# Second attention joined to the dense stage before it in one program, with the split stacks stored in rows of 4,098 bytes

## The chip, the cores and the metric

One NeuronCore of a Trainium2 chip runs the whole kernel in one launch. The metric is the device time of an execution in microseconds (us). The kernel before takes 2052.94 us (median of 3 runs, 2052.21 to 2053.58).

## What is computed

Two transformer layers over x of 8 batches x 512 positions x 128 channels, each `x = layernorm(x + f(x))` twice:

```python
x = _layernorm(x + _L0_attn_ref(...))   # relative-position attention, 16 heads of 8 channels
x = _layernorm(x + _L0_ffn_ref(...))    # r * (relu(xk W_k)^2 W_v), r = sigmoid(xr W_r)
x = _layernorm(x + _L1_attn_ref(...))   # the second attention
x = _layernorm(x + _L1_ffn_ref(...))    # gated MLP, 512 hidden units
# second attention, for each of the 16 heads of each batch:
term1 = einsum('bhqd,bhkd->bhqk', Q, K)
term2 = einsum('bhqd,kd->bhqk', Q, r)             # r: sines and cosines of the distance
term3 = einsum('hd,bhkd->bhk', u, K)[:, :, None, :]
term4 = einsum('hd,kd->hk', v, r)[None, :, None, :]
scores = (term1 + term3 + _rel_shift(term2 + term4)) / sqrt(dk)
out = einsum('bhqk,bhkd->bqhd', softmax(scores), V)
```

The shift leaves a few scores beside the diagonal that the product of split rows doesn't give; they come from a correction, the "edge" below.

## The kernel before, in words

The program is a chain of phases: `opening_phase` (projections of the first attention), `attention_phase(0)`, `mixing_phase` (output product, two layer norms, first feed-forward part, and the projections of the second attention), `attention_phase(1)` and `dense_phase`. This text calls `mixing_phase` the mixing stage. Between two phases stand two blocks of their own. `end_phase` clears every semaphore that the phase used, one instruction each on SyncE (line 89), and `start_phase` raises every semaphore of the next phase by 32, again one instruction each (line 81). Every block ends in a barrier of all engines. Each engine has its own program, written by hand in the order in which it runs; waits are on semaphores. SyncE (SP) issues all DMAs from one queue, in its program's order, and a wait on it holds back whatever is behind.

**Mixing stage.** It goes in steps (`STEPS`, from -3 to 7), and a step works on up to four batches at once: `a` (first residual), `m` (feed-forward), `p` (second norm and projections) and `tail`, the batch whose queries, keys and rotated queries are split. For `tail`, VectorE (DVE) runs `spin` and `rotate` (lines 1372 to 1381), and then three bf16 parts are made of five rows of 512 per channel: ScalarE (ACT) `high` (L1237), DVE `remainder` (L1387), ACT `middle` (L1242), DVE `low` (L1392). The halves of `full` are `HALVES[0]` (keys and both queries) and `HALVES[1]` (rotated queries). SP then stores them by `write_stacks` to `stack[1]` in HBM: 15 DMAs a batch (L1051, L1057), in rows of 512 bf16 values (1 KB), since keys and the four query arrays lie apart. `high(b, 0)` waits until the stores of batch b - 2 have landed. At its end SP waits for all stores (L1107).

**Second attention.** 128 heads, one after another, four tiles of 128 queries each. SP loads a head's rows with four DMAs (`head_load`, L532 to 535) into one of 8 slots, 8 heads ahead. TensorE (PE) makes the head's edge product (`edge`, L761), DVE copies it (`edge_out`, L848) to one of two `corr` buffers, SP writes it to `shear_e` (L577) and reads it back skewed into one of four `band` buffers (`edge_read`, L584); this is done for 5 heads before the first tile. For each tile PE makes the scores (L703, L705), DVE adds the band (`finish`, L835) and takes the row maximum (L843), ACT makes the exponentials (L906), PE turns them (L724), ACT copies them (L913). PE weighs the values for four heads at a time (L737). The first `FIRST` = 4 heads stand before the loop.

```python
            if left >= CORR_AHEAD - 1:
                hold(sp, added, 4 * (n + CORR_AHEAD - bands))
                edge_read(sp, Head(i, j + CORR_AHEAD - 1))
```

## Time and profile before

| what | value |
|---|---|
| three runs | 2052.21, 2052.94, 2053.58 us |
| the profiled execution's own time | 2053.05 us |
| its span | 2051.2 us, 44474 instructions |
| granted TensorE clock, mean | 0.937 |
| busy share of the span | PE 84%, DVE 71%, ACT 72%, POOL 4% |
| DMA | 404.65 MB, 197 GB/s over the span |

The profile comes from one execution. The first attention runs from about 105 to 897 us of the span, the mixing stage from 907 to 1085, the second attention from 1092 to 1699, the dense phase from 1704 to the end. A busy share is an average over stages that have different limits, so the rows of one stage say more than the table. In the slices of the page a digit is the busy share of a 51 us slice in tenths.

### The profile page before, as it was taken

Reading aid. Unit: us, or ns where it says so; the run is one execution under the profiler, and the core shown is the slowest. Engines: PE = TensorE matmul, PEld = TensorE weight load, DVE = VectorE, ACT = ScalarE, POOL = GpSimd, SP = SyncE. Lnnn points to the kernel's source line nnn. Section 1 sums busy time; section 2 is a strip of 40 time slices with the busy share of each in tenths; the row PEclk is TensorE's granted clock in tenths of the full one; section 3 lists DMA queues with packets and bytes.
Section 4 is the critical chain, followed back from the end, with each engine's and each line's share of the span. In section 5 each row is a group of like instructions: output and inputs, shape, how many; then the busy total and the mean of one; then the engine's idle time right before and its main releaser. Section 6 shows DMA issues by size and latency. Waiting matters only on the chain. (4 is left out here: it accounts for less than half of the span.)

```text
span 2051.2 us, 44474 instructions
## 1 busy us (share of the span) xinstructions
PE 1728.5 (84%) x11694; PEld 1042.4 (51%) x11694; DVE 1454.1 (71%) x3499; ACT 1472.5 (72%) x2600; POOL 79.9 (4%) x102
## 2 busy tenths in 40 slices
PE   5269999999999999946743999999999995999998
PEld 2045555555555555524522555656565552454544
DVE  6358888888888888837973888988888873324322
ACT  4348888888888888836862999999999991223222
POOL 0000000000000000003510000000000000000000
PEclk8569999999999999977875999999999997999999
DMA  7678888888888888726996777777777744000100
GB/s 229 214 222 257 265 269 267 264 261 266 262 264 268 266 266 261 240 56 184 327 311 182 206 213 210 215 211 214 212 211 211 212 136 117 22 20 26 36 5 11
DMA packets 428234, 404.65 MB, mean 197 GB/s; under 512 B 38169, under 2 KB 348433, under 8 KB 428049
## 3 DMA queue, kind: packets, MB, share of 16 engines
q1 hardware_dynamic: 428177, 403.99, 65.6%
q8 instruction: 24, 0.39, 0.1%
q14 instruction: 33, 0.27, 0.0%
HBM read 227.09 MB, written 176.29 MB: 197 GB/s over the span
## 5 line engine op out<-in xcount | busy, mean ns | idle before, releaser
L906 ACT ACTIVATE a_prob<-bank,a_negmax 128x512 f32<-128x512 f32 x1024 | 740.8, 723 | 47.3 <-DVE a_negmax L843 46.1
L843 DVE TENSOR_REDUCE a_negmax<-bank 128x1 f32<-128x512 f32 x1024 | 699.4, 683 | 0.3
L724 PE MATMUL bank<-a_ident,a_prob 128*128 128x128 f32 x4096 | 643.0, 280 | 56.2 <-ACT a_probt L913 48.3
L913 ACT COPY a_probt<-bank 128x512 f32<-128x512 f32 x1024 | 621.3, 607 | 90.4 <-PE bank L724 79.1
L724 PEld LDWEIGHTS bank<-a_ident,a_prob 128*128 128x128 f32 x4096 | 448.5, 141 | 171.7 <-issue 70.6
L835 DVE TENSOR_TENSOR bank<-bank,a_band 128x128 f32<-128x128 f32 (+3 forms) x1024 | 349.9, 342 | 69.6 <-PE bank L705 69.0
L703 PE MATMUL bank<-a_stks 74*128 74x192 bf16 (+7 forms) x1024 | 324.1, 317 | 10.4 <-ACT a_prob L906 10.1
L737 PE MATMUL bank<-a_probt,a_vs 128*32 128x512 f32 x2048 | 271.5, 604 | 14.9 <-ACT a_probt L913 14.9
L823 DVE COPY_PREDICATED bank<-a_mask,bank 128x128 f32<-128x128 uint32 (+1 forms) x512 | 139.6, 273 | 116.4 <-PE bank L709 114.0
L703 PEld LDWEIGHTS bank<-a_stks 74*128 74x128 bf16 (+1 forms) x1024 | 100.1, 98 | 235.3 <-ACT a_prob L906 200.4
L705 PE MATMUL bank<-a_stks 74*128 74x320 bf16 (+5 forms) x768 | 200.9, 262 | 0.0
L1676 DVE TENSOR_TENSOR d_drop<-bank,d_s 128x128 f32<-128x128 f32 x32 | 7.1, 284 | 170.4 <-PE bank L1599 170.4
L709 PE MATMUL bank<-a_stks 74*128 74x128 bf16 (+1 forms) x512 | 110.5, 216 | 10.9 <-DVE bank L823 2.6
L1578 PE MATMUL bank<-d_ha,d_h1T 128*128 128x512 f32 x256 | 112.3, 592 | 0.0
L751 PE MATMUL bank<-a_ident,a_sheared 128*128 128x128 f32 x512 | 106.4, 285 | 6.6 <-DMA a_sheared<-shear_a 5.1
L1578 PE MATMUL bank<-d_hb,d_h2T 128*128 128x512 f32 x256 | 111.2, 592 | 0.0
L925 ACT COPY a_corr<-bank 128x512 f32<-128x512 f32 x128 | 76.4, 597 | 42.9 <-PE bank L752 40.1
L848 DVE COPY a_corr<-bank 128x512 f32<-128x512 f32 x128 | 87.2, 681 | 16.7 <-PE bank L761 9.3
L752 PE MATMUL bank<-a_tabs,a_stks 65*128 65x128 bf16 x512 | 97.5, 225 | 0.0
L853 DVE COPY a_keyside<-bank 128x512 f32<-128x512 f32 x128 | 87.4, 683 | 13.3 <-PE bank L744 10.4
L761 PE MATMUL bank<-edges,a_stks 96*128 96x128 bf16 x512 | 51.0, 223 | 50.1 <-DMA a_ident<-in_ident 42.5
L1641 ACT ACTIVATE d_hb<-bank,d_fs 128x512 f32<-128x512 f32 x32 | 22.0, 687 | 90.6 <-PE bank L1578 90.6
(178 smaller groups left out, 1594.7 us busy)
## 6 DMA issues: line engine op xcount, KB each, us to landing
a_band<-shear_b SPq DMA_DIRECT2D x128, 512.0 KB, 5.0
shear_a<-a_keyside SPq DMA_DIRECT2D x128, 256.0 KB, 3.7
a_sheared<-shear_a SPq DMA_DIRECT2D x128, 256.0 KB, 3.7
shear_b<-a_corr SPq DMA_DIRECT2D x128, 256.0 KB, 2.8
shear_e<-a_corr SPq DMA_DIRECT2D x128, 256.0 KB, 2.2
a_band<-shear_e SPq DMA_DIRECT2D x128, 256.0 KB, 3.2
a_stks<-stack SPq DMA_DIRECT2D x256, 96.0 KB, 3.0
a_stks<-stack SPq DMA_DIRECT2D x384, 48.0 KB, 2.6
```

The costliest lines, as they stand in the source:

```text
L703: last = pe.matmul(score[:, 0:c], k[:, qlo, q], k[:, keys, 0:c], start=True, stop=True)
L705: last = pe.matmul(score[:, c:T], k[:, qhi, q], k[:, keys, c:T], start=True, stop=True)
L709: last = pe.matmul(other[:, 0:e - a], k[:, qhi, q], k[:, keys, a:e], start=True, stop=True)
L724: last = pe.transpose(turned_bank[k][:, n * 128:(n + 1) * 128], prob[h.slot % 2][:, n, k * 128:(k + 1) * 128], ident[:, :])
L737: pe.matmul(cbank[32 * j:32 * j + VW, :], vs[g][:, at:at + VW], probt[h.slot + j][:, k, :], start=(k == 0), stop=(k == NT - 1)).then_inc(p ...
L751: pe.matmul(corr_bank[:, q], sheared[h.slot % 4][:, q], ident[:, :], is_transpose=True, start=True, stop=False)
L823: v.copy_predicated(score[:, a:e], mask[:, 0:e - a], other[:, 0:e - a]).then_inc(fixed, 1)
L835: v.tensor_tensor(score[:, a:e], score[:, a:e], band[h.slot % bands][:, n, w:w + e - a], ALU.add).then_inc(added, 1)
L843: v.tensor_reduce(negmax[h.slot % 2][:, n:n + 1], score[:, :], AX.X, ALU.max, negate=True).then_inc(maxed, 1)
L906: nc.scalar.activation(prob[h.slot % 2][:, n, :], score[:, :], ACT.Exp, bias=negmax[h.slot % 2][:, n:n + 1]).then_inc(exped, 1)
L913: nc.scalar.copy(probt[h.slot][:, k, :], turned_bank[k][:, :]).then_inc(copied, 1)
L1578: last = pe.matmul(dst[:, :], w[:, k, 128 * m:128 * m + 128], src[:, k, :], start=(k == 0), stop=(k == KH - 1))
```

## The change

The mixing stage and the second attention become one block with one `start_phase` ahead of it and one `end_phase` behind it. `mixing` and `attention` are now functions that give back a `Stage`, whose `program` writes the engines' parts one behind the other into the same block. To fit in memory, most tiles of the mixing stage lie in an `arena` whose bytes the attention's `prob` and `probt` tiles use later. Bands and `corr` buffers of the second attention are 8 and 8 instead of 4 and 2. The first 5 heads' edge products, copies (now on ACT), writes and reads, the first 8 heads' loads, the key positions and the first values are issued inside the mixing steps. The last batch's stacks are stored between the attention's first four heads (`store_last`), and SP waits for all stores of the mixing stage (`settled`) before the attention's loop. `stack[1]` is laid out anew: keys first, then both queries and both rotated queries side by side, so that a batch is stored by 3 DMAs of 1 KB rows and 3 DMAs of 4,098-byte rows instead of 15 of 1 KB rows; a row of the stack is 5,184 bytes from the next instead of 5,120.

```diff
-ARRAYS = 5
+PITCH_S = 5 * T + 32
...
-                wide, bands = WIN if rel else REL, 4
+            wide, bands, corrs = (WIN, 4, 2) if rel else (REL, 8, 8)
...
+            def edge(pe, h, target):
+                pe.wait_ge(stk_in[h.slot], BASE + per_stk * (h.i + 1))
...
+            def first_edge(pe, j):
+                pe.wait_ge(corr_copied, BASE + j - 1)
+                edge(pe, Head(0, j), first_banks[j % 2])
+            def first_edge_out(act, j):
+                act.wait_ge(corr_mm, BASE + j + 1)
+                nc.scalar.copy(corr[j][:, :, :], first_banks[j % 2][:, :].rearrange("p (n r) -> p n r", n=NT)).then_inc(corr_copied, 1)
...
                         for j in range(FIRST):
                             sync_step(sp, 0, j, NHEAD, weighed=False)
+                        if not rel:
+                            mix.store_last(sp, j)
+                    if not rel:
+                        mix.settled(sp)
...
                     @block.tensor
                     def _(pe):
                         if not rel:
-                            pe.wait_ge(s_const, BASE + 16)
-                        if not rel:
-                            for j in range(CORR_AHEAD):
-                                edge(pe, Head(0, j))
+                        mix.banks_free(pe)
                             pe.wait_ge(poskey_in, BASE + 16)
...
-                        else:
-                            for j in range(CORR_AHEAD):
-                                edge_out(v, Head(0, j))
...
+            def write_queries(sp, b, run):
+                sp.wait_ge(lo_set, BASE + 2 * b + 2)
+                first_term, n, q = TERM_RUNS[run]
+                same = bass.AP(part[b % 2][:, :, :].tensor, q * (WIDE + 2) + QV, [[3 * (WIDE + 2), C], [0, n], [1, 4 * T + 1]])
+                sp.dma_start(stack[1][b, :, first_term:first_term + n, T:5 * T + 1], same).then_inc(stack_written[b % 2], 16)
+            def store_last(sp, j):
+                if j < len(TERM_RUNS):
+                    write_queries(sp, B - 1, j)
+                else:
+                    write_keys(sp, B - 1)
+            def banks_free(pe):
+                for done in (q_out, qs_out, key_out, v_out, relu_done, summed1, turn2, gated):
+                    pe.wait_ge(done, BASE + B)
...
                             if p is not None:
                                 store_rows(p)
+                        if tail == 6:
+                            for j in range(CORR_AHEAD):
+                                att.edge_write(sp, j)
                             if tail is not None:
                                 write_values(tail)
-                                write_stacks(tail)
+                        if tail == 6:
+                            for j in range(CORR_AHEAD - 1):
+                                att.edge_read(sp, j)
+                        if tail == 7:
+                            att.edge_read(sp, CORR_AHEAD - 1)
+                        if tail is not None and tail < B - 1:
+                            write_keys(sp, tail)
+                            for run in range(len(TERM_RUNS)):
+                                write_queries(sp, tail, run)
+                        if tail == 1:
+                            att.first_poskey(sp)
+                        if tail == 2:
+                            sp.wait_ge(v_written[0], BASE + 16)
+                            sp.wait_ge(stack_written[0], BASE + 16 * N_STACK)
...
+                            att.first_values(sp)
+                        if tail in (2, 3, 4, 5):
+                            att.head_load(sp, 2 * tail - 4)
+                            att.head_load(sp, 2 * tail - 3)
```

In the step with `tail` = 6, PE runs `first_edge` 2 and 3 behind `flip_rows2` and `first_edge` 4 between `queries` and `keys`; `first_edge` 0 and 1 end the step before. ACT runs `first_edge_out` 0 and 1 behind `rows2`, 2 and 3 behind `turned2`, and 4 behind `middle(6, 0)`.

Two places in the order of the instructions. On ACT, in the step with `tail` = 6, the kernel before has (L1258 is `rows2` of batch 7, L1237 `high`, L1270 `turned2`, L1242 `middle`, L1210 to L1214 `queries_out`):

```order
L1258 ACTIVATE m_x21<-m_pre2,m_shift,m_rstd 128x128 x4
L1237 CAST m_part0<-m_full0 128x1024
L1270 COPY m_xt2<-bank5 128x512
L1242 CAST m_part0<-m_left 128x1538
L1210 ACTIVATE m_qv<-bank0,m_uvs 128x512
L1211 ACTIVATE m_full1<-bank0,m_uvs 128x512
L1214 ACTIVATE m_full1<-bank1,m_uvs 128x512
L1242 CAST m_part0<-m_left 128x1024
```

and the changed kernel, whose mixing tiles are named after the arena they lie in:

```order
L1322 ACTIVATE m_x21<-arena,m_shift,m_rstd 128x128 x4
L655 COPY a1_corr0<-bank6 128x512
L655 COPY a1_corr1<-bank4 128x512
L1301 CAST m_part0<-arena 128x1024
L1334 COPY arena<-bank5 128x512
L655 COPY a1_corr2<-bank6 128x512
L655 COPY a1_corr3<-bank4 128x512
L1306 CAST m_part0<-arena 128x1536
L655 COPY a1_corr4<-bank6 128x512
L1274 ACTIVATE arena<-bank0,m_uvs 128x512
L1275 ACTIVATE arena<-bank0,m_uvs 128x512
L1278 ACTIVATE arena<-bank1,m_uvs 128x512
```

Five copies have come in ahead of `queries_out`. On SP, at the end of the mixing stage, the kernel before stores the last batch and goes through the change of phase (L89 clears semaphores) to the first head's load:

```order
L1051 DMA stack1<-m_part1 128x512
L1057 DMA stack1<-m_part1 128x512 x4
L1017 UNCONDITIONAL_BRANCH
L86 UNCONDITIONAL_BRANCH
L89 ISA x67
L85 UNCONDITIONAL_BRANCH
L78 UNCONDITIONAL_BRANCH
L77 UNCONDITIONAL_BRANCH
L629 UNCONDITIONAL_BRANCH
L532 DMA a1_stks<-stack1 48x1536
```

and in the changed kernel the edge writes and reads of the first heads stand in the mixing step with `tail` = 6, ahead of that batch's stores (L1035 keys, L1042 queries):

```order
L1097 DMA resid<-m_x21 128x4x128
L582 DMA shear_e<-a1_corr0 128x4x128
L582 DMA shear_e<-a1_corr1 128x4x128
L582 DMA shear_e<-a1_corr2 128x4x128
L582 DMA shear_e<-a1_corr3 128x4x128
L582 DMA shear_e<-a1_corr4 128x4x128
L1092 DMA values<-m_vt0 128x4x144
L589 DMA a1_band0<-shear_e 128x4x128
L589 DMA a1_band1<-shear_e 128x4x128
L589 DMA a1_band2<-shear_e 128x4x128
L589 DMA a1_band3<-shear_e 128x4x128
L1035 DMA stack1<-m_part0 128x3x512
```

The loads of the first eight heads have moved further up, to the steps with `tail` = 2 to 5, behind those steps' stores.

## Rows read from the trace of the kernel before

**Rows 1.** The page, part 1: busy time of each engine over the span.
```profile
PE 1728.5 (84%) x11694; PEld 1042.4 (51%) x11694; DVE 1454.1 (71%) x3499; ACT 1472.5 (72%) x2600; POOL 79.9 (4%) x102
```
**Rows 2.** Windows: start:end, length, busy by engine, then PEclk, DMA share, GB/s.
```profile
1060.00:1070.00 10.00, 0.00 (x0) 0.00 (x0) 7.95 (x8) 4.94 (x4) 0.00 (x0) 0.51 0.99 338
1110.00:1120.00 10.00, 7.03 (x32) 4.29 (x33) 7.41 (x18) 5.47 (x9) 0.00 (x0) 0.50 0.85 230
1300.00:1400.00 100.00, 94.55 (x788) 60.45 (x784) 88.89 (x203) 98.45 (x185) 0.00 (x0) 1.00 0.73 214
```
**Rows 3.** Timeline of DVE at the change of phase: start, us, line, operation, idle before.
```profile
1057.32 1.23 DVE L1392 TENSOR_TENSOR m_part<-m_left,m_part 128x1024 bf16<-128x1024 f32 x1 [2.12 <-ACT m_part L1242]
1058.46 0.68 DVE L1372 TENSOR_TENSOR m_rot<-m_qv,m_trig 128x512 f32<-128x512 f32 x1
...
1065.49 2.90 DVE L1392 TENSOR_TENSOR m_part<-m_left,m_part 128x1538 bf16<-128x1538 f32 x2 [0.41 <-ACT m_part L1242]
1092.45 0.11 DVE L858 MEMSET a_vs<- 128x23 f32 x2 [24.07 <-PEq L77]
...
1112.68 0.49 DVE L835 TENSOR_TENSOR bank<-bank,a_band 128x128 f32<-128x128 f32 x2
```
**Rows 4.** Clears (L89) and increments (L81) of semaphores on SP at two changes of phase.
```profile
L81 SPq EVENT_SEMAPHORE  x67: 17/17/17, 903.0 to 906.9; - x67
L89 SPq EVENT_SEMAPHORE_RANGE_CLEAR  x67: 25/25/29, 1085.9 to 1089.5; - x67
```
**Rows 5.** Timeline of DVE, first `spin` product of two steps that follow each other.
```profile
1000.69 0.69 DVE L1372 TENSOR_TENSOR m_rot<-m_qv,m_trig 128x512 f32<-128x512 f32 x1
1015.87 0.69 DVE L1372 TENSOR_TENSOR m_rot<-m_qv,m_trig 128x512 f32<-128x512 f32 x1
```
**Rows 6.** Timeline of ACT in the step with tail 6, and `high(7, 0)` behind it.
```profile
1047.79 1.65 ACT L1258 ACTIVATE m_x<-m_pre,m_shift,m_rstd 128x128 f32<-128x128 f32 x4 [0.66 <-POOL m_shift L1313]
1050.26 1.04 ACT L1237 CAST m_part<-m_full 128x1024 bf16<-128x1024 f32 x1 [0.83 <-DVE m_full L1381]
1053.96 0.69 ACT L1210 ACTIVATE m_qv<-bank,m_uvs 128x512 f32<-128x512 f32 x1 [0.55 <-PE bank L1155]
1056.25 1.03 ACT L1242 CAST m_part<-m_left 128x1024 bf16<-128x1024 f32 x1
1060.15 1.47 ACT L1237 CAST m_part<-m_full 128x1538 bf16<-128x1538 f32 x1 [1.46 <-DMA stack<-m_part]
```
**Rows 7.** Timeline of PE: queries of batch 7, an edge product at the same clock.
```profile
1051.85 2.07 PE L1155 MATMUL bank<-m_xt,m_wq 128*128 128x512 f32 x2 [1.25 <-ACT m_xt L1270]
1053.71 1.92 PE L1157 MATMUL bank<-m_xt,m_wqs 128*128 128x512 f32 x2
1101.93 0.61 PE L761 MATMUL bank<-edges,a_stks 96*128 96x128 bf16 x4 [0.79 <-DVE a_corr L848]
```
**Rows 8.** The page, part 5: an ACT copy of 128x512 out of PSUM.
```profile
L913 ACT COPY a_probt<-bank 128x512 f32<-128x512 f32 x1024 | 621.3, 607 | 90.4 <-PE bank L724 79.1
```
**Rows 9.** Timeline of SP: first store of batch 5, batch 7's residual, last stores.
```profile
1046.52 0.37 SPq L1051 DMA_DIRECT2D stack<-m_part  x1
...
1058.06 0.46 SPq L1061 DMA_DIRECT2D resid<-m_x  x1
...
1081.71 2.19 SPq L1057 DMA_DIRECT2D stack<-m_part  x4
```
**Rows 10.** Windows: 1 KB stores alone, opening stores with rows to 6 KB, 512-byte zeros.
```profile
1070.00:1083.00 13.00, 0.00 (x0) 0.00 (x0) 0.00 (x0) 0.00 (x0) 0.00 (x0) 0.50 1.00 342
49.00:52.00 3.00, 2.53 (x4) 0.70 (x5) 2.96 (x5) 1.26 (x3) 0.00 (x0) 0.65 1.04 407
936.00:941.00 5.00, 4.94 (x28) 3.50 (x26) 2.93 (x11) 2.64 (x4) 2.54 (x4) 0.86 1.05 291
```
**Rows 11.** The page, part 6: band reads, KB each, us from issue to landing.
```profile
a_band<-shear_e SPq DMA_DIRECT2D x128, 256.0 KB, 3.2
```
**Rows 12.** One tile (a_stks), 1085 to 1140 us: issue time in ns, min/median/max.
```profile
L533 SPq DMA_DIRECT2D a_stks<-stack x12: 414/424/2032, 1092.8 to 1137.5; - x12
```

More of the change, by code:

```diff
@@ L415, in _, with attention @@
                         offset_low(B - 1)
-        def attention_phase(layer, kept=None):
+        class Stage:
+            pass
+        def attention(layer, ctx, kept):
             rel = layer == 0
@@ new lines, in attention @@
+            else:
+                arena, ident = kept
+                stks = sb("stks", [R1, unroll, 4, T], BF16)
+                tiles = arena.rearrange("p (i n t) -> p i n t", n=NT, t=T)
+                prob, probt = [tiles[:, i] for i in range(2)], [tiles[:, 2 + i] for i in range(unroll)]
+            stk = [stks[:, i] for i in range(unroll)]
+            vs = [sb(f"vs{i}", [128, GROUP * NT * VC + VW - VC]) for i in range(vslots)]
+            negmax = [sb(f"negmax{i}", [128, NT]) for i in range(2)]
@@ new lines, in attention @@
+            outs = sb("outs", [128, T])
+            wide, bands, corrs = (WIN, 4, 2) if rel else (REL, 8, 8)
+            corr = [sb(f"corr{i}", [128, NT, REL]) for i in range(corrs)]
+            band = [sb(f"band{i}", [128, NT, wide]) for i in range(bands)]
+            if rel:
+                mask = sb("mask", [128, 128], U32)
+                tab = [tabs[:, i] for i in range(unroll)]
+                keyside = [sb(f"keyside{i}", [128, T]) for i in range(4)]
+                sheared = [sb(f"sheared{i}", [128, T]) for i in range(4)]
@@ new lines, in first_poskey, with first_values @@
+            def first_poskey(sp):
+                every = bass.AP(waves[:, :].tensor, 0, [[T, SR], [0, unroll], [1, T]])
+                sp.dma_start(stks[SR:R1, :, KEY, :], every).then_inc(poskey_in, 16)
+            def first_values(sp):
+                for g in range(vslots):
+                    sp.dma_start(vs[g][:, 0:GROUP * NT * VC], values[g]).then_inc(v_in[g], 16)
+            def edge(pe, h, target):
+                pe.wait_ge(stk_in[h.slot], BASE + per_stk * (h.i + 1))
+                for n in range(NT):
+                    q = slice(128 * n, 128 * n + 128)
+                    last = pe.matmul(target[:, q], stk[h.slot][:, EDGE, q], edges[:, :], start=True, stop=True)
+                last.then_inc(corr_mm, 1)
@@ new lines, in scalar_step @@
+                            if left >= (k + exp_ahead) // NT:
+                                exp_tile(act, *ahead(i, j, k, exp_ahead))
+                            copy_turned(act, own, k)
+                            if k == 1 and weighed and j % GROUP == GROUP - 1:
+                                group_out(act, Head(i, j - j % GROUP - GROUP))
+                        if rel and left >= CORR_AHEAD:
+                            corr_out(act, Head(i, j + CORR_AHEAD))
+                    for j in range(FIRST):
+                        scalar_step(0, j, NHEAD, weighed=False)
@@ new lines, in _ @@
+                    with act.Fori(0, loops) as i:
+                        for j in range(unroll):
+                            scalar_step(i, FIRST + j, NHEAD)
+                    for j in range(last):
+                        scalar_step(loops, FIRST + j, last - 1 - j)
+                    group_out(act, Head(loops, FIRST + last - GROUP))
+            stage = Stage()
+            stage.head_load, stage.edge_write, stage.edge_read = ((lambda sp, j, move=move: move(sp, Head(0, j)))
+                                                                  for move in (head_load, edge_write, edge_read))
@@ L1719, in build @@
             end_phase()
-            attention_phase(0, kept)
-            end_phase()
-        mixing_phase()
-        end_phase()
-        attention_phase(1)
+            with ExitStack() as ctx:
+                att = attention(0, ctx, kept)
+                start_phase()
+                with nc.Block() as block:
+                    att.program(block)
+            end_phase()
+        with ExitStack() as ctx:
+            arena = ctx.enter_context(nc.sbuf_tensor("arena", [128, (2 + UNROLL[1]) * NT * T], F32))
+            ident = ctx.enter_context(nc.sbuf_tensor("ident", [128, 128], F32))
+            att = attention(1, ctx, (arena, ident))
+            mix = mixing(ctx, arena, ident, att)
+            start_phase()
+            with nc.Block() as block:
+                mix.program(block)
+                att.program(block, mix)
         end_phase()
```

1661 lines of the change are left out of this document (818 added, 843 removed).

## The prediction

> **What bounds the kernel now.** I read the page first: PE is busy for 84% of the span, DVE and ACT for some 72% [rows 1], so there is idle time, and the question is where. The windows give it by stage. Inside the second attention ACT is busy for 98.45 of 100 us at a granted clock of 1.00 (2.4 GHz) [rows 2]: that stage is ACT's, and nothing in the change makes ACT's work there shorter. Between 1060 and 1070 us PE is idle, DVE and ACT finish the last split, and DMA is at 0.99 of its share [rows 2]. The timeline of DVE then shows the hole: the last `low` of the mixing stage ends at 1065.49 + 2.90 = 1068.39, and the first tile of the second attention is finished from 1112.68 on, **44.3 us** later [rows 3]. In that hole lie the stores of the last two batches (to 1083.9) [rows 9], the clears and increments of semaphores [rows 4], the loads of the first heads and their edge corrections. DVE and ACT stand on both sides of it, so the hole is on the path whole.
>
> Inside the mixing stage the steps follow each other every 15.2 us [rows 5]. DVE has hardly a gap there, and DMA is nearly full too, so I treat both as limits and check below which of them the changed kernel meets.
>
> **1. The hole goes: -44.3 us, +0.2.** The second attention's programs now stand behind the mixing stage's in the same block. DVE goes from its last `low` to two memsets (0.11 us together [rows 3]) and the first `finish`. That one needs four things: PE's scores (banks free once ACT has copied batch 7's values, about 10 us earlier), the loaded heads and key positions (issued two to five steps earlier), and band 0. I find all of them ready; band 0 is the latest, and is worked out in part 3. The ramp behind the first tile has the same work as before. PE went through it at a granted clock of 0.50, 1.2 GHz, after the idle stretch at 0.51 [rows 2], and I expect the same again.
>
> **2. Five edge copies on ACT: +3.1 us.** They came off DVE's start of the attention, inside the hole, and now stand ahead of `queries_out` in the step with `tail` = 6. ACT was at 1.04 us of cast from 1050.26, and started `queries_out` at 1053.96 [rows 6]. A copy takes 0.61 us [rows 8]. Copies 0 and 1 fit mostly into the 0.83 us in which ACT waited for DVE; `turned2` then ends at about 1052.2. PE, at 0.61 us for an edge product, runs edge 2 and 3 before `queries`, starts these at 1052.2 and, as their two products took 2.07 and 1.92 us from 1051.85 on [rows 7], reaches edge 4 at about 1056.2 and ends it at 1056.8. Copy 4 waits for that on ACT, and `queries_out` for copy 4: start at 1057.5. Three activations of 0.6 on, the second `middle` starts at 1059.4, where it was at 1056.25 [rows 6]: +3.1. DVE's `low` waited for exactly this one (2.12 us [rows 3]), and all of DVE's work for batch 7 follows it, so it is on the path. Bounds: 0, if PE is faster and ACT's waits hide the copies; 4.5, five copies and an edge product and a half. The rest of `tail` = 7 keeps its length. The 1.46 us that ACT waited for a store before `high(7, 0)` [rows 6] was not on the path: DVE was busy until 1062.
>
> **3. The stores and what SP now carries: 0 us.** A batch's stack is 15 DMAs or 3840 KB, 3.93 MB. SP issues them at the pace at which they flow: 1046.5 to 1058.0, 11.5 us [rows 9], or 342 GB/s in the stretch with stores of 1 KB rows alone [rows 10]. Four fifths of the bytes (3.15 MB) now go in rows of 4,098. The nearest rows are the opening phase's stores, in rows of 1 to 6 KB: 407 GB/s [rows 10]. I take 400, which gives 7.9 us for these and 2.3 us for the keys at 342: 10.2 us a batch, 1.3 less. The lower bound is the 291 GB/s of 512-byte zeros and loads [rows 10]: 13.5 us a batch, 2.0 more.
> In the steps 2 to 5 SP has eight more issues each, for two heads. At 0.42 to 0.5 us [rows 12] that is 3.8 us, more than their bytes need. Stores, loads and the residual and value DMAs (1.0 us) make 15.0 us, just under the 15.2 of the step. So store 5 starts about where it did, 0.5 us late, ends at 1057.2 and SP is through the loads at 1061. `high(7, 0)`, now at 1061.6, doesn't wait. Residual, five edge writes and the values take 3.3 us more. The read of band 0 goes out at about 1064.8 and, with 3.2 us to landing [rows 11] and a full queue, lands by 1069. DVE arrives at 1071.5. So the cover is 2.5 us; when it is gone, what is late next is band 0, and behind it `high(7, 0)`.
> Band 4 is read a whole store later, near 1076, but is due only 16 tiles on. The last batch's stack (3.93 MB) goes out during four heads of about 5.9 us, which carry some 0.8 MB of their own each: 7.1 MB at 342 are 21 us in 23.6. Bands are read four heads ahead; I cost it at nothing.
>
> **4. Semaphores: +6.7 us.** The instructions that clear and raise them don't go away; the hole only held some of them. The merged program has 109 semaphores (67 and 42; the attention alone had 32). Increments cost 3.9 us for 67, or 0.059 each, and clears 3.6 us for 67, or 0.054 [rows 4]. Ahead of the mixing stage there are 42 more: +2.5. Behind the attention there are 77 more clears: +4.2. Both stand where all engines wait.
>
> **5. Edits costed at nothing.** DVE's edge copies with 8 buffers instead of 2 wait less, in a stage that ACT bounds. The far rotated rows are read in 1 KB rather than 2 KB pieces, under a DMA share of 0.73 [rows 2]. `settled` on SP waits some 3 us, with bands and heads several heads ahead. The arena changes addresses, not instructions.
>
> **Sum.** -44.3 + 0.2 + 3.1 + 0 + 6.7 = -34.3 us against the profiled execution's 2053.05 us: **2018.8 us**. The median of the runs is 0.1 us lower, so no correction is due.
>
> **The rivals.**
> *A. DMA holds the mixing stage's end: the long rows are no faster.* For it: DMA is already at 0.99 to 1.00 of its share there [rows 2, 10]. Against it: 407 GB/s in the opening. At 342 each store is 1.3 us longer; over the steps 1 to 5, with SP's extra issues, store 5 starts 4 us late, band 0 lands near 1074 instead of 1069, and DVE waits 2.5: 2021.3. At 291, store 5 ends at 1070, `high(7, 0)` is late too and band 0 lands at 1082: 2029.3. The Trainium skill, DMA: Bandwidth & Descriptors, section "Where 436 GB/s comes from", says that for transfers between HBM and SBUF a core's share of HBM, about 358 GB/s, binds. By that rule this rival would hold, near its first time. The trace disagrees for short stretches: 3 us at 407 GB/s.
> *B. The attention starts on time but starves.* Stores of batch 7 delay the head loads and bands on SP's one queue. The last band before the stores has a slack of many us, the bytes fit only at 90%. If one head's worth of work is lost: +5.9, 2024.7.
> *C. Slower than before: the 4,098-byte rows are slow ones.* Their last 2 bytes are a piece of their own kind, and rows begin on multiples of 64 bytes only. Six stores stand ahead of band 0 on SP's queue, and the step has no room left, so each us more per store costs six. The change loses once they take 34.3 / 6 = 5.7 us more each, 3.15 MB in 13.6 us, or 231 GB/s. At half of the measured 342 they take 18.4 us, band 0 comes 55 us later than I have it, and the time is about 2073. Against it: no row moves that slowly in a full queue; even 512-byte pieces reach 291.
> *D. The overlap doesn't come about.* Some wait (the banks, the key positions) holds the attention back to the end of all stores, near 1084: 12 us lost, 2031. Against it: the code's waits name only batch-7 products that are ten us old.
>
> **How the numbers follow.** Forecast (parts 1 to 4, DMA with cover) 0.62; A at 342 to 291 0.18; B 0.08; D 0.07; C 0.05. The forecast's own bounds are 2015.7 (edge copies free) and 2020.2 (copies at 4.5), and PE may come into the ramp nearer its last work and at the higher clock, which I put at 1 to 2 us less: 2014. The range goes to 2028, over B and most of A, and leaves out D, C and the worst of A: about 0.15. All cases but C are faster by over 0.2% (4 us, about what a measurement of this kernel tells from no change): faster 0.95, within 0.2% 0.01, slower 0.04.
>
> **What would show it.** Right: DVE's gap between the last `low` and the first `finish` under 1 us; `queries_out` of batch 7 behind copy 4, 3 us later against `rows2` of batch 7; stores of a batch in 10 us; 109 increments over 6.4 us ahead of the mixing stage and 109 clears over 5.9 behind the attention; the attention's steady stage unchanged at ACT 98%. Wrong: a wait for `a_band` or for `stack<-m_part` at the joint (A), mixing steps longer than 15.2 us (A or C), ACT under 95% in the first heads (B), or a gap of over 10 us on DVE (D).

## The result, and the profile after

The changed kernel takes **2025.26 us** (median of 4 runs, 2023.52 to 2025.86), against 2053.01 for the kernel before beside it: ratio 0.9862, 95% interval 0.9849 to 0.9875. Faster, as forecast, and inside the range, but 27.8 us are gained where the forecast was 34.3. The profiled execution (2025.06 us, span 2023.3, granted clock 0.945) is the one read here.

I cut both executions at the same places. "Ahead" reaches from SP's first clear behind the first attention to the first of the last eight `spin`s, "mixing" from there to the end of the last `low`, "gap" to the first `finish`, "attention" to SP's first clear behind it, "rest" to the end of the span.

| us | opening, first attention | ahead | mixing | gap | second attention | rest | span |
|---|---|---|---|---|---|---|---|
| before | 899.7 | 54.2 | 114.5 | 44.3 | 587.3 | 351.2 | 2051.2 |
| after | 899.1 | 56.5 | 117.2 | 0.0 | 593.4 | 357.1 | 2023.3 |
| difference | -0.6 | +2.3 | +2.8 | -44.3 | +6.1 | +5.9 | -27.9 |

The timeline of DVE over the change of program (start, us, line, operation, idle before it) answers [rows 3]:

```profile
1061.80 1.23 DVE L1464 TENSOR_TENSOR m_part<-arena,m_part 128x1024 bf16<-128x1024 f32 x1 [3.46 <-ACT m_part L1306]
1062.94 0.69 DVE L1444 TENSOR_TENSOR arena<-arena 128x512 f32<-128x512 f32 x1
...
1069.97 2.90 DVE L1464 TENSOR_TENSOR m_part<-arena,m_part 128x1536 bf16<-128x1536 f32 x2 [0.40 <-ACT m_part L1306]
...
1072.84 0.27 DVE L838 TENSOR_TENSOR bank<-bank,a_band 128x128 f32<-128x128 f32 x1
```

The hole of 44.3 us is gone to the last tenth: the first `finish` (L838) starts at 1072.84, as the last `low` (L1464) ends. But 20 us on, DVE stands still, and again behind that (same columns):

```profile
1094.80 0.30 DVE L838 TENSOR_TENSOR bank<-bank,a_band 128x128 f32<-128x128 f32 x1 [3.12 <-DMA a_band<-shear_e]
1100.52 0.30 DVE L838 TENSOR_TENSOR bank<-bank,a_band 128x128 f32<-128x128 f32 x1 [1.84 <-PE bank L719]
1112.50 0.30 DVE L838 TENSOR_TENSOR bank<-bank,a_band 128x128 f32<-128x128 f32 x1 [3.63 <-DMA a_band<-shear_e]
```

It waits for bands 5 and 8 to land (heads are counted from 0, four `finish` each). SP's timeline shows where they were (issues, us, line; the waits of SP are the gaps between rows):

```profile
1085.44 0.43 SPq L1042 DMA_DIRECT2D stack<-m_part  x1
1086.83 0.38 SPq L582 DMA_DIRECT2D shear_e<-a_corr  x1
1087.33 1.30 SPq L589 DMA_DIRECT2D a_band<-shear_e  x1
...
1101.49 1.68 SPq L1035 DMA_DIRECT2D stack<-m_part  x3
1107.25 0.37 SPq L582 DMA_DIRECT2D shear_e<-a_corr  x1
1108.00 0.37 SPq L589 DMA_DIRECT2D a_band<-shear_e  x1
```

Band 5's read (L589) is issued at 1087.33, behind a store of 1,537 KB (L1042) of 1085.44, and DVE has it 7.5 us later. Band 8's read comes after the stores of the keys and after `settled`, in which SP waited for all stores of the stack (the waits of SP's queue, 1072 to 1130: us in total, times, longest):

```profile
SPq L522 <- DVE a_corr L851: 9.5, 5, 6.4
SPq L1057 <- DMA stack<-m_part: 3.6, 1, 3.6
```

The windows (PE, PEld, DVE, ACT busy us and instructions, POOL, granted clock, DMA share, GB/s) show what it does to ACT, which bounds this stage. They answer to [rows 2]:

```profile
1080.00:1090.00 10.00, 9.46 (x70) 6.16 (x67) 9.22 (x23) 9.86 (x19) 0.00 (x0) 0.98 0.97 333
1090.00:1100.00 10.00, 7.21 (x43) 3.25 (x43) 5.56 (x13) 7.53 (x14) 0.00 (x0) 0.87 1.05 327
...
1110.00:1120.00 10.00, 6.84 (x46) 4.00 (x44) 5.71 (x14) 5.57 (x11) 0.00 (x0) 0.83 0.73 209
1300.00:1400.00 100.00, 94.08 (x783) 59.73 (x782) 88.11 (x202) 98.11 (x185) 0.00 (x0) 1.00 0.73 212
```

9.86 of 10 us while the bands that were read in the mixing stage last, 7.53 and 5.57 in the two windows with the waits, and 98 of 100 later, as in the kernel before. PE's clock falls to 0.87 and 0.83 in the windows in which it ran dry.

The semaphores stand as counted (one line of code: duration ns, first and last start; increments L81, clears L89), to be read beside [rows 4]:

```profile
L81 SPq EVENT_SEMAPHORE  x109: 17/17/17, 902.4 to 909.1; - x109
L89 SPq EVENT_SEMAPHORE_RANGE_CLEAR  x109: 25/25/49, 1666.2 to 1672.7; - x109
```

6.7 and 6.5 us. And ACT in the step with `tail` = 6, which answers to [rows 6]:

```profile
1050.18 1.65 ACT L1322 ACTIVATE m_x<-arena,m_shift,m_rstd 128x128 f32<-128x128 f32 x4 [0.66 <-POOL m_shift L1385]
1051.73 1.04 ACT L655 COPY a_corr<-bank 128x512 f32<-128x512 f32 x2
...
1054.10 1.07 ACT L655 COPY a_corr<-bank 128x512 f32<-128x512 f32 x2
1055.05 1.49 ACT L1306 CAST m_part<-arena 128x1536 bf16<-128x1536 f32 x1
1058.50 0.58 ACT L655 COPY a_corr<-bank 128x512 f32<-128x512 f32 x1 [1.96 <-PE bank L646]
1058.98 0.69 ACT L1274 ACTIVATE arena<-bank,m_uvs 128x512 f32<-128x512 f32 x1
```

From `rows2` to `queries_out` ACT takes 8.80 us, 6.17 before, and most of the difference is the wait of 1.96 us for edge product 4 on PE.

### The profile page after: what moved, and what is told of

It is laid out like the page before. It is cut to its first block and busy times, and to the rows that moved or that the text cites. A ratio compares the mean times of both kernels' runs of the same rounds, so it can differ in the third digit from the quotient of the medians.

```text
span 2023.3 us, 44383 instructions
## 1 busy us (share of the span) xinstructions
PE 1729.5 (85%) x11694; PEld 1041.1 (51%) x11694; DVE 1449.1 (72%) x3492; ACT 1473.1 (73%) x2605; POOL 79.5 (4%) x102
## 5 line engine op out<-in xcount | busy, mean ns | idle before, releaser
L838 DVE TENSOR_TENSOR bank<-bank,a_band 128x128 f32<-128x128 f32 (+3 forms) x1024 | 350.0, 342 | 76.6 <-PE bank L719 69.5
L906 ACT ACTIVATE arena<-bank,a_negmax 128x512 f32<-128x512 f32 x512 | 376.5, 735 | 7.7 <-DVE a_negmax L846 7.1
L906 ACT ACTIVATE a_prob<-bank,a_negmax 128x512 f32<-128x512 f32 x512 | 359.7, 702 | 26.0 <-DVE a_negmax L846 25.4
L738 PE MATMUL bank<-a_ident,a_prob 128*128 128x128 f32 x2048 | 329.8, 284 | 42.4 <-ACT a_probt L913 42.0
L913 ACT COPY a_probt<-bank 128x512 f32<-128x512 f32 x512 | 300.9, 588 | 79.0 <-PE bank L738 66.8
L738 PE MATMUL bank<-ident,arena 128*128 128x128 f32 x2048 | 314.5, 276 | 14.2 <-ACT arena L913 7.2
L913 ACT COPY arena<-bank 128x512 f32<-128x512 f32 x512 | 316.2, 618 | 13.9 <-PE bank L738 13.8
L738 PEld LDWEIGHTS bank<-ident,arena 128*128 128x128 f32 x2048 | 233.4, 142 | 72.5 <-issue 42.8
L738 PEld LDWEIGHTS bank<-a_ident,a_prob 128*128 128x128 f32 x2048 | 216.3, 141 | 102.4 <-ACT a_probt L913 50.1
L751 PE MATMUL bank<-arena,a_vs 128*32 128x512 f32 x1024 | 137.5, 611 | 14.0 <-ACT arena L913 14.0
L751 PE MATMUL bank<-a_probt,a_vs 128*32 128x512 f32 x1024 | 136.6, 608 | 0.8 <-ACT a_probt L913 0.8
```

Of the source, the lines that this page charges most:

```text
L738: last = pe.transpose(turned_bank[k][:, n * 128:(n + 1) * 128], prob[h.slot % 2][:, n, k * 128:(k + 1) * 128], ident[:, :])
L751: pe.matmul(cbank[32 * j:32 * j + VW, :], vs[g][:, at:at + VW], probt[h.slot + j][:, k, :], start=(k == 0), stop=(k == NT - 1)).then_inc(p ...
L838: v.tensor_tensor(score[:, a:e], score[:, a:e], band[h.slot % bands][:, n, w:w + e - a], ALU.add).then_inc(added, 1)
L906: nc.scalar.activation(prob[h.slot % 2][:, n, :], score[:, :], ACT.Exp, bias=negmax[h.slot % 2][:, n:n + 1]).then_inc(exped, 1)
L913: nc.scalar.copy(probt[h.slot][:, k, :], turned_bank[k][:, :]).then_inc(copied, 1)
```

## The experiments

The kernel before ran beside each series, with medians of 2052.1 to 2055.3 us, so I lean on the profiled stages, which separate what the whole time mixes. Each stage time is that of one execution. The five kernels whose mixing stage is the changed kernel's, instruction by instruction (it, settled_later, spread_stores, sems_shared and after_again), have 116.5 to 118.6 us there: a difference of 1 or 2 us in that stage between two profiles shows nothing.

| kernel | median us (lowest to highest) | ahead | mixing | gap | second attention | rest |
|---|---|---|---|---|---|---|
| settled_later | 2019.80 (2016.37 to 2023.40) | 56.7 | 116.5 | 0.0 | 588.3 | 355.8 |
| spread_stores | 2017.51 (2016.98 to 2020.50) | 56.6 | 118.6 | 0.0 | 586.5 | 356.6 |
| merged_1kb | 2034.28 (2033.67 to 2036.31) | 56.6 | 122.9 | 2.3 | 596.6 | 357.2 |
| layout_only | 2047.64 (2044.52 to 2049.96) | 54.4 | 113.4 | 41.9 | 586.7 | 351.8 |
| edges_on_dve | 2020.75 (2019.54 to 2023.82) | 56.4 | 116.8 | 0.0 | 594.9 | 356.9 |
| sems_shared | 2006.14 (2004.08 to 2007.66) | 50.7 | 117.0 | 0.0 | 594.1 | 350.8 |
| loads_later | 2029.52 (2027.49 to 2031.45) | 56.4 | 124.3 | 0.0 | 594.5 | 356.7 |
| all_four | 2003.23 (2001.26 to 2004.40) | 50.9 | 121.0 | 0.0 | 586.6 | 350.9 |
| best | 1999.74 (1997.64 to 2003.67) | 51.4 | 114.4 | 0.0 | 586.9 | 351.5 |
| after_again | 2025.59 (2023.81 to 2027.26) | 56.4 | 118.3 | 0.0 | 593.8 | 356.6 |
| best_again | 2000.78 (1998.34 to 2003.20) | 51.1 | 114.0 | 0.0 | 588.4 | 351.3 |

**1. The starved heads: two kernels that move SP's last work.**

```
-                    if not rel:
-                        mix.settled(sp)
-                    with sp.Fori(0, loops) as i:
+                    for j in range(0 if rel else unroll):
+                        sync_step(sp, 0, FIRST + j, NHEAD)
+                    if not rel:
+                        mix.settled(sp)
+                    with sp.Fori(0 if rel else 1, loops) as i:
```

> Changed kernel, but SP's wait for all stores of the mixing stage stands 8 heads later (its first loop iteration is peeled). Theory S (the missing 6 us are lost in the attention's first heads, because SP's one queue holds bands back): DVE's second wait, 3.6 us for band 8, goes and the first one, 3.1 us for band 5, stays, so 2 to 3.5 us less than the changed kernel's 2025.3: about 2022.5. Rival R (the ramp is slower for another reason, such as TensorE's clock or the stage being ACT's): no change, 2025.3, even if DVE no longer waits there.

Measured: 2019.80. The second wait is gone and the first is left; this is the whole of DVE's waits for bands between 1072 and 1200 us (columns: us in total, times, longest):

```profile
DVE bank L840 <- DMA a_band<-shear_e: 3.2, 1, 3.2
```

The attention takes 588.3 us instead of 593.4: 5.1 less, and the whole time is 5.5 less, more than the 2 to 3.5 I gave it. Theory S holds for the place, R falls. But a wait of 3.6 us cost about 5, and the one of 3.1 that is left costs only 1.0 against the 587.3 of before.

The second kernel keeps that and cuts the stores up, one a head, over nine heads instead of four:

```
+                        mix.store_last(sp, FIRST + j)
...
-                if j < len(TERM_RUNS):
-                    write_queries(sp, B - 1, j)
-                else:
-                    write_keys(sp, B - 1)
+                b, w = B - 1, part[(B - 1) % 2]
+                if j == 0:
+                    sp.wait_ge(lo_set, BASE + 2 * B)
+                if j < NTERM:
+                    q = Q_PART[j]
+                    sp.dma_start(stack[1][b, :, j, T:5 * T + 1], w[:, q, QV:QV + 4 * T + 1]).then_inc(stack_written[b % 2], 16)
+                elif j < NTERM + len(TERM_RUNS):
+                    first_term, n, q = TERM_RUNS[j - NTERM]
+                    sp.dma_start(stack[1][b, :, first_term:first_term + n, 0:T], w[:, 0:n, KEYS:KEYS + T]).then_inc(stack_written[b % 2], 16)
```

> As settled_later, and the last batch's stack goes out in nine DMAs of at most 512 KB, one a head, instead of six in four heads. Theory S: both waits for bands go, first finish to the first clear of a semaphore takes 587.3 to 588.3 us as in the kernel before (593.3 in the changed one), in all 5 to 6 us less than the changed kernel: 2019.3 to 2020.3. Rival R: that stretch stays at 593 us and the time at 2025.3. Rival Q (it is the volume of the stores beside the heads, not their place in the queue): half of it is left, 2022.

Measured: 2017.51, attention 586.5, both a little below what I gave them. Of DVE's waits for bands one of 0.7 us is left, and ACT is nearly full in the three windows from 1090 us on, though DMA carries 304 GB/s on their average against 254 in the changed kernel (windows of spread_stores, columns as above):

```profile
1090.00:1100.00 10.00, 9.25 (x68) 5.62 (x69) 8.48 (x20) 9.73 (x19) 0.00 (x0) 1.00 0.93 287
1100.00:1110.00 10.00, 9.75 (x82) 5.82 (x82) 9.45 (x22) 10.00 (x20) 0.00 (x0) 1.00 1.06 308
1110.00:1120.00 10.00, 9.09 (x79) 5.88 (x76) 8.07 (x20) 9.64 (x19) 0.00 (x0) 1.00 1.06 318
```

So the same bytes cost nothing once no band stands behind a large store or behind `settled`. Rival Q, the volume, falls for the greater part: settled_later leaves the stores beside the same four heads and gives 5.1 us back. The last 1.8 us could be its own, since spread_stores halves the volume beside each head as well. What starved the heads was mainly order on SP's one queue, not the amount of data.

**2. What the long rows are worth: one kernel on either side.** The first gives the changed kernel its stores in 1 KB rows back:

```
-                same = bass.AP(part[b % 2][:, :, :].tensor, q * (WIDE + 2) + QV, [[3 * (WIDE + 2), C], [0, n], [1, 4 * T + 1]])
-                sp.dma_start(stack[1][b, :, first_term:first_term + n, T:5 * T + 1], same).then_inc(stack_written[b % 2], 16)
+                for at, size in ((QV, T), (QU, T), (ROT0, T), (ROT1, T + 1)):
+                    same = bass.AP(part[b % 2][:, :, :].tensor, q * (WIDE + 2) + at, [[3 * (WIDE + 2), C], [0, n], [1, size]])
+                    sp.dma_start(stack[1][b, :, first_term:first_term + n, at:at + size], same).then_inc(stack_written[b % 2], 16)
```

> Changed kernel, but every store of the stack is in rows of 1 KB (15 DMAs a batch, as before), nothing else undone. If long rows move faster, as forecast (400 against 342 GB/s), a batch takes 1.3 us more here, 9 more issues stand on SP in each step, and DVE waits for band 0 or the steps get longer: 2027 to 2030. If rows of 1 KB and of 4 KB cost the same: 2025.3 within 1 us. Rival L (the long rows are what holds up small transfers, since they are accepted far ahead of the flow): this one is faster, 2021 to 2023.

Measured: 2034.28, 9 us more than the changed kernel and above what I gave it. The mixing stage is 5.7 us longer, its step from the fifth to the sixth `spin` 19.28 us instead of 17.05. ACT's `high` now waits for stores again and again (waits in merged_1kb, 1015 to 1080: us in total, times, longest), where the changed kernel has one such wait of 2.0 us in the whole stage:

```profile
ACT m_part L1302 <- DMA stack<-m_part: 8.8, 4, 3.3
```

At the joint DVE now waits for band 0 (timeline of DVE in merged_1kb):

```profile
1074.03 2.89 DVE L1465 TENSOR_TENSOR m_part<-arena,m_part 128x1536 bf16<-128x1536 f32 x2 [0.40 <-ACT m_part L1307]
1076.88 0.11 DVE L861 MEMSET a_vs<- 128x23 f32 x2
1079.27 0.50 DVE L838 TENSOR_TENSOR bank<-bank,a_band 128x128 f32<-128x128 f32 x2 [2.28 <-DMA a_band<-shear_e]
```

That is rival A of the prediction, nearly as I described it, in the kernel without long rows. Another 3.2 us lie in the attention. Rival L, that the whole is faster without the long rows because they hold small transfers up, falls: small transfers do land later behind them (last section), but the kernel is slower without them. In the changed kernel (windows of 15 us, columns as above) and in merged_1kb, the same stretches:

```profile
1000.00:1015.00 15.00, 11.69 (x58) 8.03 (x58) 14.83 (x32) 13.01 (x23) 8.68 (x9) 0.89 1.05 351
1015.00:1030.00 15.00, 10.38 (x49) 6.96 (x50) 11.76 (x29) 11.00 (x19) 6.80 (x7) 0.89 1.06 359
1030.00:1045.00 15.00, 10.51 (x45) 6.73 (x44) 10.87 (x20) 12.47 (x20) 3.90 (x4) 0.77 1.01 347
```

```profile
1000.00:1015.00 15.00, 11.55 (x58) 7.93 (x58) 14.12 (x31) 13.05 (x22) 7.94 (x9) 0.89 1.05 324
1015.00:1030.00 15.00, 9.65 (x38) 6.35 (x39) 9.41 (x23) 9.18 (x16) 5.14 (x6) 0.77 0.97 302
1030.00:1045.00 15.00, 9.58 (x47) 6.91 (x46) 10.02 (x17) 11.36 (x20) 4.84 (x4) 0.77 0.96 301
```

351, 359 and 347 GB/s against 324, 302 and 301, at a DMA share of about 1 in both. The mixing stage is DMA's here, and DVE's busy time falls with it. Divided by the DMA share these are 334 to 344 GB/s against 309 to 314, some 9%. The two kernels also differ in the number of DMAs, 6 against 15 a batch, and in the time SP needs to issue them; no run separates that from the length of the rows.

The second puts the new layout and its six stores a batch into the kernel before, phases apart:

```
-                N_STACK = ARRAYS * len(TERM_RUNS)
+                N_STACK = 2 * len(TERM_RUNS)
...
+                            for first_term, n, q in TERM_RUNS:
+                                same = bass.AP(part[b % 2][:, :, :].tensor, q * (WIDE + 2) + QV, [[3 * (WIDE + 2), C], [0, n], [1, 4 * T + 1]])
+                                sp.dma_start(stack[1][b, :, first_term:first_term + n, T:5 * T + 1], same).then_inc(stack_written[b % 2], 16)
```

> Kernel before, with the new layout of the stack and its six stores a batch alone, phases apart. If long rows move at 400 GB/s, the stores of two batches that end in the hole between the phases end 2 to 3 us earlier: 2050.0 to 2051.0 against 2053.0. If all rows cost the same: 2053.0 within 0.5 us. Rival C of the prediction (the 4,098-byte rows are slow): over 2055.

Measured: 2047.64, 5.2 us less than before and 2.4 below what I gave it. The hole is 41.9 instead of 44.3 us, the 2 to 3 expected; the mixing stage is 1.1 shorter, where I expected nothing, and 1.2 lie in the first attention, whose code is untouched. Differences that small in one profile each show nothing by themselves; what is shown is the whole time, and in it the 2.4 us of the hole. Rival C, slow long rows, falls.

**3. The edge copies.** Copies 2, 3 and 4 go from ACT to DVE:

```
...
                             remainder(tail, 1)
+                            if tail == 6:
+                                att.first_edge_out_v(v, 2)
+                                att.first_edge_out_v(v, 3)
                             low(tail, 0)
+                            if tail == 6:
+                                att.first_edge_out_v(v, 4)
                             low(tail, 1)
```

> Changed kernel, but three of the five edge copies (2, 3, 4) are made by DVE, two ahead of batch 6's first low and one ahead of its second, where DVE waited 1.15 and 3.46 us for ACT. If ACT is what lengthens the step after batch 6's (14.14 us from spin to spin, 12.05 in the kernel before), that step falls to 12.1 to 12.7 and the time by 1.5 to 2.5 us, to 2023 to 2024. Rival: DVE has no room for them, or DMA bounds that step: 14.1 us and 2025.3, as now.

Measured: 2020.75. The step is 12.08 us, as before the change. DVE's timeline shows the copies (L656) in what had been idle time:

```profile
1054.76 1.41 DVE L656 COPY a_corr<-bank 128x512 f32<-128x512 f32 x2
1056.08 1.75 DVE L1466 TENSOR_TENSOR m_part<-arena,m_part 128x1536 bf16<-128x1536 f32 x1
1057.99 0.69 DVE L656 COPY a_corr<-bank 128x512 f32<-128x512 f32 x1 [0.15 <-PE bank L646]
1059.14 1.23 DVE L1466 TENSOR_TENSOR m_part<-arena,m_part 128x1024 bf16<-128x1024 f32 x1 [0.47 <-ACT m_part L1311]
```

So the copies' place on ACT was worth 2.1 us. The whole time fell by 4.5, but its profiled run has a mixing stage of 116.8 us, because two earlier steps are longer (16.52 and 17.82 us for 14.94 and 17.05), and is no faster than the changed kernel outside the first attention; I hold only the 2.1 to be shown.

**4. The semaphores.** All five engines share them:

```
+        def share(block, act_on):
+            for k, engine in enumerate((block.sync, block.scalar, block.gpsimd, block.vector, block.tensor)):
+                @engine
+                def _(q, k=k):
+                    for handle in list(sems.values())[k::5]:
+                        act_on(q, handle)
...
-                @block.sync
-                def _(sp):
-                    for handle in sems.values():
-                        sp.sem_clear(handle)
+                share(block, lambda q, handle: q.sem_clear(handle))
```

> Changed kernel, but the semaphores are raised ahead of each phase and cleared behind it by all five engines, a fifth each, instead of by SP alone. The changed trace has 258 increments in 15.6 us and 222 clears in 13.5 us, all with the other engines waiting. If their price is SP's own pace (0.06 us each), four fifths of 29 us go, less what the first 65 hid: 2002 to 2006; around the merged part 13.2 us become 2.6 to 3.5. Rival: the price is that of a path all engines share, so five engines are no faster: 2025.3.

Measured: 2006.14, 19.1 us less, at the near end of the expectation. The stretch up to the first clear behind the first attention shrinks by 6.1 us, the part ahead of the mixing stage by 5.8 and the rest by 6.3. The 109 clears take 2.6 us, from 1654.7 to 1657.3, and PE is the last (one line of code, columns as above; PEld is PE's queue):

```profile
L91 POOLq EVENT_SEMAPHORE_RANGE_CLEAR  x22: 44/44/44, 1654.7 to 1656.5; - x22
L91 SPq EVENT_SEMAPHORE_RANGE_CLEAR  x22: 25/25/49, 1654.8 to 1656.0; - x22
L91 PEldq EVENT_SEMAPHORE_RANGE_CLEAR  x21: 56/56/56, 1654.9 to 1657.3; - x21
```

From one clear to the next that is 0.06 us on SP, 0.09 on POOL and 0.12 on PE, so the other engines are slower, but they work side by side. PE is slower at raising too: its 21 increments of the 109 take 3.1 us. So the two lists around the merged part, 13.2 us in the changed kernel, still take 5.8 and not the 2.6 to 3.5 expected. The price of the lists was SP's own pace, not that of a path all engines share, and it was on the path.

**5. The loads of the first heads, one step later.**

```
-                        if tail in (2, 3, 4, 5):
-                            att.head_load(sp, 2 * tail - 4)
-                            att.head_load(sp, 2 * tail - 3)
+                        if tail in (3, 4, 5):
+                            att.head_load(sp, 2 * tail - 6)
+                            att.head_load(sp, 2 * tail - 5)
```

(Heads 6 and 7 are loaded ahead of the first edge write of step 6.)

> Changed kernel, but the loads of the first heads begin one step later (heads 0 to 5 in the steps 3 to 5, heads 6 and 7 at the start of step 6): 0.67 MB less go out ahead of store 5, nothing is left out. If DMA's backlog is what makes the steps after batch 3's and batch 4's 17.1 and 16.0 us (15.2 to 15.5 and 15.0 in the kernel before), the two together get 1.5 to 2.5 us shorter and the time is 2023 to 2024. Rival: those steps are of the engines' own making, or the loads only press later: no change, 2025.3.

Measured: 2029.52, a miss on the wrong side. The two steps that the expectation names are those from the fifth `spin` to the sixth and on to the seventh. They take 17.72 and 15.00 us, together 0.3 less. The first is no matter of these loads: the store that `high(4, 0)` waits for is issued ahead of them. The second may be, but after_again has 15.04 there with the loads unmoved. And the step with `tail` = 6 grows from 14.14 to 19.72, since edge 4 needs head 4, which was now loaded behind store 5 (PE in loads_later):

```profile
1062.50 0.58 PE L646 MATMUL bank<-edges,a_stks 96*128 96x128 bf16 x4 [5.42 <-DMA a_stks<-stack]
```

**6. Together.**

> Changed kernel with the spread stores and the late wait of spread_stores, DVE's edge copies, the later loads and the shared semaphores together. If the four causes add: 2017.5 less 23, less 2, less 2: 1990 to 1996. If the first three press on the same DMA queue and only one of them counts: 1995 to 1999.

Measured: 2003.23, above both ranges. It holds the later loads, whose harm the same series showed: its mixing stage takes 121.0 us. Without them:

> Changed kernel with the spread stores and the late wait, DVE's three edge copies and the shared semaphores, the first heads' loads where the changed kernel has them. If the three gains add, as each was alone against 2025.3 (7.8 for the stores, 2.1 to 4.5 for the edges, 19.1 for the semaphores): 1994 to 1996, and 7 to 9 us less than with the later loads (2003.2), whose step after batch 6's took 17.3 us where this one should take 12.1. Rival: the gains overlap on DMA's queue and 2 to 5 us of them are lost: 1997 to 2001.

Measured: 1999.74; 3.5 us less than all_four instead of 7 to 9, and 4 more than the sum of the whole times said. By stages it does add: against the changed kernel's 767.1 us from clear to clear it has 752.7, made of 5.1 ahead, 2.8 in mixing and 6.5 in the attention. Its profiled run had 802.5 us in the first attention (first clear to first clear) where all_four had 797.9. The two kernels to compare, once more and side by side:

> The changed kernel once more, beside best_again on one chip, as the base of the sums: 2023 to 2026 if its first four runs (2023.5 to 2025.9) show its whole spread. If the first attention, which varied by 5 us between the profiles of kernels that share it (797.9 to 802.5 us), makes the spread, its runs reach from 2020 to 2026, and the stretch from the first clear behind that attention to the first clear behind the second is 767 us within 1 us again.

> The kernel best once more, beside after_again on one chip. Its first profile had 752.7 us from the first clear behind the first attention to the first clear behind the second, against 767.1 in the changed kernel, but a first attention of 802.5 us. If only that attention varies: 1997 to 2001, 24 to 27 us under after_again.

Measured side by side: 2025.59 and 2000.78, 24.8 us apart, ratios to the kernel before 0.9852 (0.9834 to 0.9871) and 0.9735 (0.9719 to 0.9751). The stretch from clear to clear is 768.5 and 753.5, so the changed kernel's is 1.4 us longer than in its first profile. The first attention is 803.1 and 799.9 by the same count, but that count holds 65 clears and 48 increments, which best_again shares out. From the last of these increments to the first clear it is 796.1 and 796.7, alike in the two. The changed kernel's runs reach from 2023.81 to 2027.26 and not down to 2020, so nothing here shows that the first attention makes the spread. **best** is faster than both kernels, by 2.65% than the one before.

## Why the prediction was right or wrong

**The hole (-44.3, +0.2): right.** Measured -44.3, and the memsets cost nothing beside it. No wait holds the first `finish`, so rival D did not occur. Band 0's read went out at 1066.15, 1.3 us later than I had it, and DVE came at 1072.84, also 1.3 later. That it was ready is a close thing: in merged_1kb it came 2.3 us late.

**The edge copies (+3.1): the mechanism right, the size a third of itself too high.** Wait by wait it is what I worked out: copy 4 held by edge 4 on PE, `queries_out` behind it by 2.6 us. The step grew by 2.1; the half microsecond between the two isn't explained. Experiment 3 gives exactly the 2.1 back.

**Stores and SP (0): right in sum, too optimistic in its parts.** The mixing stage grew by 2.8 us, 2.1 of them the edges, so 0.7 stays for this part (1.8 in after_again), which is within what that stage varies by. My own sign for rival A, steps longer than 15.2 us, did show: from the fifth `spin` to the sixth and on to the seventh it is 17.05 and 16.00 us, 15.51 and 15.03 before, and three earlier steps of 14.9 (15.2, 16.25 and 15.18 before) make up for it. The sum may hide two larger terms: the 15 stores of 1 KB rows made the stage 5.7 us longer, so the first heads' data would have cost about that much without the long rows. I had priced rival A's ordinary rows at 2.5 us; its test cost 9.0, because I charged a late store only to band 0 and not to the steps, in which `high` waits for the store of two batches back (8.8 us of waits in experiment 2), nor to the heads behind. The rule that I set against my figure (the Trainium skill, DMA: Bandwidth & Descriptors, section "Where 436 GB/s comes from": about 358 GB/s) lies near what a whole step moves, 351, 359 and 347 GB/s. As a ceiling it doesn't hold here: 10 us at the joint move 388, and the measurement decides:

```profile
1070.00:1080.00 10.00, 4.59 (x20) 2.87 (x21) 9.54 (x21) 7.48 (x11) 0.00 (x0) 0.50 1.07 388
```

So 400 GB/s was near the truth for a stretch that is mostly stores and wrong for the step, and it is steps that count there.

One sum of the prediction is wrong, with nothing hanging on it: in rival C six stores that take 10.5 us longer each are 63 us late, not 55.

**Semaphores (+6.7): right, slightly low.** 109 increments take 6.7 us where 67 took 3.9 (+2.8), 109 clears 6.5 where 32 took 1.7 (+4.8): +7.6.

**What failed: "Bands are read four heads ahead; I cost it at nothing."** This is rival B, which I gave 0.08 and priced at 5.9; the attention is 6.1 us longer, and its time, 2024.7, was the measured one within 0.6 us. Its sign, ACT under 95% in the first heads, showed as 75% and 56%. Its price was luck, and so is part of the hit: the time lies in my range because I had drawn the range over B. The step has three errors in it. I took 5.9 us for a head, but 587.3 us for 128 heads are 4.6. I took the distance from the edge product to its use for SP's freedom: the product of head j+5 is copied out at the end of step j, its read goes out in the step behind, and DVE wants the band about one head after that. Band 5's read went out at 1087.33, and DVE was ready for it at 1091.68, 4.4 us on; in the steady stage, near 1400 us, it takes a band up 4.6 to 5.5 us after its read is issued. And I compared bytes with time (7.1 MB in 23.6 us) where the question was what stands ahead of one small read on SP's queue: a store of 1.5 MB once, and `settled`, which I had costed at "some 3 us, with bands and heads several heads ahead" and which took 3.6 us of SP from a band that had no such lead. Experiment 1 takes away first the second wait and then nearly all of the first (0.7 us is left), and gives all 6.1 us back.

By the terms, with what lies outside them: -44.3 hole, +2.1 edges, +0.7 stores, +7.6 semaphores, +6.1 starved heads, -0.1 in all else (the first attention -0.6, the ahead part -0.5 beside its increments, the last part +1.1 beside its clears) make -27.9, the difference of the spans. The forecast had -34.3; 6.1 of the 6.4 us missing are the starved heads.

**Left open.** Why the first 3 us of waits for bands cost next to nothing and the next 4 cost 5 to 6. DVE's waits for bands over the whole attention, against its length, both in us: 0.2 and 587.3 in the kernel before, 0.7 to 2.9 and 586.5 to 586.9 in spread_stores, best and all_four, 3.2 and 588.3 in settled_later, 3.6 and 588.4 in best_again, 6.7 to 9.9 and 593.4 to 594.9 in the five other merged kernels with long rows. A head start used up by the first waits would explain it, but no run separates that. Also open is why one mixing program has a step of 17 to 18 us in some executions and none over 16.3 in another (settled_later); it moves the stage by 1 to 2 us. In the changed kernel `high(4, 0)` waits 2.0 us for a store in that step, and settled_later has 0.2 us of such waits in its whole stage, so the stores are near it, but what makes them late in one execution and not in the other isn't shown. Experiment 5, whose step was 17.72 us with the loads moved, speaks against the head loads.

## What to carry to other kernels

When a barrier is taken away, look past the joint: work that the barrier had put alone now stands in front of small, urgent transfers on the same queue. For each of those, find the instruction that releases it and the one that needs it, and count what the queue holds in between; sums of bytes hide it. Large last stores belong one at a time between the urgent ones, and a wait for their end as late as anything allows. And where phases are set up by one engine while the others wait, that list is worth dividing before anything finer: here it was 19 us.

## What the runs showed of the hardware that was not expected

- In the changed kernel, with its larger transfers, SP is free earlier and the data lands later. Medians from issue to landing between 985 and 1034 us: the loads of x took 4.3 us in the kernel before, 4.2 in merged_1kb and 10.3 in the changed kernel; SP issued a batch's six stores in 5.4 us (1000.92 to 1006.32), the last of which landed near 1017.4. Fifteen smaller ones held it for 11.5 us [rows 9]. The wait moves from SP into the queue, and a small urgent transfer issued behind it waits there.
- With 6 stores a batch, half of them in rows of 4,098 bytes begun at multiples of 64 bytes, a full stretch of 15 us moves 347 to 359 GB/s; with 15 stores in rows of 1 KB the same kernel moves 301 to 324 (merged_1kb).
- A semaphore's clear takes 0.06 us on SP, 0.09 on POOL and 0.12 on PE, and five engines do it side by side: 109 clears in 2.6 us instead of 6.5 (sems_shared).
- The first attention, the same code in all of these kernels, took 792.8 to 799.3 us by the profiles (last increment ahead of it to first clear behind it). That spread is as large as most effects studied here, and why the stages were compared rather than the whole times.
